# Complex products moved to GpSimd, constants set in the first stage, and an up product with stationary weights, in a two-layer state space, attention and mixture kernel

## What is computed

```
# 1. state space tokens: x holds C (8 batches x 256 channels x 64 states, complex)
dtA = A * dt[:, None];  dA = (1 + dtA/2) / (1 - dtA/2)
K   = 2 * Re( einsum('chn,hnl->chl', C * B, dA ** arange(256)) )
# 2. attention with causal mask, 3. attention and a mixture of experts by position,
# 4. gated linear attention, each with a layer norm behind it
# 5. mixture of experts: 8 experts, the best 2 for each token
h      = relu(x @ W1[e] + b1[e])           # 256 -> 1024
expert = h @ W2[e] + b2[e]                 # 1024 -> 256
out    = sum over the top 2 of expert * softmax(the two gate scores);  layernorm(x + out)
```

## Time and profile before

| what | value |
|---|---|
| median of 3 runs | 1494.32 us (1494.07 to 1497.88) |
| profiled execution, its own time | 1494.08 us |
| span of that execution | 1492.3 us |
| PE busy | 1115.6 us (75% of the span) |
| DVE busy | 695.7 us (47%) |
| ACT busy | 490.5 us (33%) |
| POOL busy | 144.6 us (10%) |
| mean granted TensorE clock | 0.833 of full speed |
| `s4_tokens`, from the start to the next block | 0 to 116.0 us |
| `main_loop` | 116.0 to 1029.9 us |
| main loop's constants | GpSimd 116.0 to 123.5 us, DVE 122.4 to 128.1 us |
| `expert_mixture` | 1029.9 us to the end; its 39 tiles from 1117 to 1436 us |

### The profile page before, as it was taken

The page is one execution under the profiler, slowest core; times in us unless marked ns, Lnnn a source line. Parts: engine busy times, 40 slices in busy tenths (PEclk is TensorE's granted clock), DMA queues, the critical chain, the costliest instruction groups (busy, mean ns, idle before and its releaser), DMA issues. The chain is left out here.

```text
span 1492.3 us, 21826 instructions
## 1 busy us (share of the span) xinstructions
PE 1115.6 (75%) x7926; PEld 745.1 (50%) x7926; DVE 695.7 (47%) x1686; ACT 490.5 (33%) x989; POOL 144.6 (10%) x211
## 2 busy tenths in 40 slices
PE   1134977987988888988879886773309999999940
PEld 0022655544764456763547554643306676676630
DVE  6972345664535766457674664243302222222227
ACT  2211232444543533454435442420002323333310
POOL 3741000000000000000000000000160000000035
PEclk9566896986989987899869987975559999999975
DMA  8011010000022000020001100103940101101114
GB/s 259 15 34 48 15 51 22 16 15 1 2 64 70 1 15 15 29 92 1 1 15 63 58 1 15 57 0 135 380 162 22 36 29 36 36 29 36 33 53 127
DMA packets 65480, 77.99 MB, mean 52 GB/s; under 512 B 14961, under 2 KB 57601, under 8 KB 65249
## 3 DMA queue, kind: packets, MB, share of 16 engines
q1 hardware_dynamic: 61040, 63.08, 13.2%
q0 software_dynamic: 4336, 13.50, 2.8%
HBM read 55.86 MB, written 20.71 MB: 51 GB/s over the span
## 5 line engine op out<-in xcount | busy, mean ns | idle before, releaser
L1463 DVE TENSOR_REDUCE mx<-scores_ps 128x4 f32<-128x1024 f32 (+1 forms) x160 | 187.1, 1169 | 140.4 <-PE scores_ps L947 93.4
L1286 ACT ACTIVATE pt<-turned_ps 128x1024 f32<-128x1024 f32 (+1 forms) x160 | 157.9, 987 | 148.3 <-PE turned_ps L969 102.8
L1908 PE MATMUL x_ps<-x_w,x_xtT 128*128 x312 | 143.5, 603 | 0.9 <-ACT x_xtT L1948 0.6
L1919 PE MATMUL x_ps<-x_w,x_hT 128*128 x624 | 141.2, 379 | 2.1 <-ACT x_hT L1963 2.1
L2054 DVE COPY x_raw<-x_ps 128x512 f32<-128x512 f32 x78 | 54.0, 692 | 168.4 <-PE x_ps L1908 168.4
L1963 ACT ACTIVATE x_hT<-x_ps,x_b1c 128x128 f32<-128x128 f32 x312 | 85.0, 383 | 142.0 <-PE x_ps L1926 142.0
L1919 PEld LDWEIGHTS x_ps<-x_w,x_hT 128*128 128x128 f32 x624 | 115.6, 190 | 16.8 <-issue 2.7
L959 PE MATMUL turned_ps<-q,k 32*128 32x256 f32 x512 | 73.7, 363 | 25.4 <-DVE mx L1463 14.7
L897 POOL COPY vpad<-v 128x64 f32<-128x64 f32 x64 | 17.3, 301 | 743.2 <-PE ps L1008 597.5
L959 PEld LDWEIGHTS turned_ps<-q,k 32*128 32x128 f32 x512 | 45.8, 210 | 84.3 <-issue 48.3
L1908 PEld LDWEIGHTS x_ps<-x_w,x_xtT 128*128 128x128 f32 x312 | 57.3, 194 | 59.2 <-issue 59.2
(11 more groups left out here) (360 smaller groups left out, 1991.1 us busy)
## 6 DMA issues: line engine op xcount, KB each, us to landing
wexp<-in_L_ffn_w SPq DMA_DIRECT2D x16, 1024.0 KB, 5.5
x_w<-in_L_ffn_W SPq DMA_DIRECT2D x16, 1024.0 KB, 13.8
x_slots<-s_zero POOLq DMA_DIRECT2D x1, 4992.0 KB, 19.3
x_xt<-x_slots SPq DMA_DIRECT2D x39, 128.0 KB, 2.2
y_slots<-x_y SPq DMA_DIRECT2D x39, 128.0 KB, 1.7
ha<-h SPq DMA_DIRECT2D x16, 256.0 KB, 3.1
h<-s_out SPq DMA_DIRECT2D x32, 64.0 KB, 1.8
x<-hb SPq DMA_DIRECT2D x8, 256.0 KB, 2.5
```

What stands on the lines that cost most here:

```text
L1286: sc.activation(pt[v.index // 2 % (PT_RING // 2)][:, :, 0:wide], turned_ps[:, :, 0:wide], ACT.Exp)\
L1463: v.tensor_reduce(mx[:, u.group % 2, 0:blocks, u.n:u.n + 2].rearrange("p b n -> p n b"), scores_ps[:, :, 0:blocks * (P if u.causal else T) ...
L1908: last = mm(ps[h][:, :], xtT[:, i % 2, c, :], w1[:, bass.ds(expert, 1), c, h * HALF:(h + 1) * HALF], start=c == 0, stop=c == DC - 1)
L1919: last = mm(ps[4 + (i - 1) % 2][:, 0:D], hT[:, (i - 1) % 2, f, :], w2[:, bass.ds(last_expert, 1), f, :], start=f == 0, stop=f == FT - 1)
```

## The change

There are three parts.

**State space step.** DVE no longer makes the imaginary part of `cb`. It signals `discrete` when `da` is ready; TensorE turns the two blocks of `da` alone, and DVE reads the result from PSUM into `dk[0]` (the buffer `dat` is gone). GpSimd waits until all eight squares are there, doubles B, and makes both parts of `cb`; TensorE turns them four blocks at a time, and ACT copies four at once. The zero fill of the scatter buffer follows behind them. The last block of the output is stored by ACT instead of SP.

**Constants.** The class `Constants` holds the buffers; GpSimd fills them behind its last group of columns, DVE prepares weights and selection matrices behind its last group of powers. The buffer `v0[1]`, which shares its place with others, is still set in the main loop. The activation table is loaded at the start.

**Mixture.** DVE copies the 128 x 2048 values of the tile's `w1` into one of two buffers `w1s`, two tiles ahead. TensorE takes 128 x 128 blocks of it as stationary and the 128 columns of `xtT` as moving, so the up result comes out turned: 16 matmuls for a tile into banks 0 and 1, or 2 and 3. The 8 transposes and the copies to `raw` are gone, and ACT reads the up product's banks itself.

```diff
+    def by_vector(self, dve, v, ident, wt):
+        s = Counted(dve, self.steps)
+        dve.wait_ge(wt.loaded, 16 * len(wt.loads))
...
+        dve.wait_ge(self.in_place, 1)
...
+        dve.sem_inc(self.ready, 1)
@@ s4_tokens, gpsimd
             pool.wait_ge(loaded, 16 * NLOAD)
+            pool.wait_ge(x_loaded, 16 * HF)
+            pool.wait_ge(squares, 8)
             g_.tensor_scalar(bin_[:, :, :, :], bin_[:, :, :, :], 2.0, None, ALU.mult).then_inc(doubled, 1)
             pool.wait_ge(doubled, 1)
-            pool.wait_ge(x_loaded, 16 * HF)
-            s.mark(g_.tensor_tensor(cb_part(0), xr, br, ALU.mult))
-            s.step(g_.tensor_tensor(ct[0][:, :, :, :], xi, bi, ALU.mult))
-            g_.tensor_tensor(cb_part(0), cb_part(0), ct[0][:, :, :, :], ALU.subtract).then_inc(prepared, 1)
+            for i, (u, w, op) in enumerate(((br, bi, ALU.subtract), (bi, br, ALU.add))):
+                s.mark(g_.tensor_tensor(cb_part(i), xr, u, ALU.mult))
+                s.step(g_.tensor_tensor(ct[i][:, :, :, :], xi, w, ALU.mult))
+                g_.tensor_tensor(cb_part(i), cb_part(i), ct[i][:, :, :, :], op).then_inc(prepared, 1)
...
-            pool.wait_ge(squares, 8)
...
+            consts.by_pool(pool, g_, ident)
@@ s4_tokens, scalar, behind the last copy
+            n = HF * NG - 1
+            act.wait_ge(copied, n + 1)
+            for j in range(J):
+                t0 = P + (NG - 1) * GT + j * TI
+                act.dma_start(h0[t0:t0 + TI].rearrange("t c (a b) -> (c a) t b", b=NB),
+                              out[n % 4][j * M:(j + 1) * M, :, :]).then_inc(stored[n % 4], 16)
@@ expert_mixture, tensor
-                    if i:
-                        pe.wait_ge(sg("raw"), 2 * i)
-                    for h in range(2):
+                    pe.wait_ge(sg("w1_now"), i + 1)
+                    if i >= 2:
+                        pe.wait_ge(sg("hT"), FT * (i - 1))
+                    for f in range(FT):
                         for c in range(DC):
-                            last = mm(ps[h][:, :], xtT[:, i % 2, c, :],
-                                      w1[:, bass.ds(expert, 1), c, h * HALF:(h + 1) * HALF],
-                                      start=c == 0, stop=c == DC - 1)
-                        last.then_inc(sg("up_full"), 1)
+                            last = mm(ps[2 * (i % 2) + f // KH][:, f % KH * P:(f % KH + 1) * P],
+                                      w1s[:, i % 2, c, f * P:(f + 1) * P],
+                                      xtT[:, i % 2, c, :], start=c == 0, stop=c == DC - 1)
+                        if f % KH == KH - 1:
+                            last.then_inc(sg("up_full"), 1)
...
-                if i < TILES:
-                    for h in range(2):
-                        pe.wait_ge(sg("raw"), 2 * i + h + 1)
-                        for k in range(KH):
-                            last = tr(ps[2 + h][:, k * P:(k + 1) * P], raw[:, h, k * P:(k + 1) * P], ident[:, :])
-                        last.then_inc(sg("hT_full"), 1)
@@ expert_mixture, vector
+            def take_w1(i):
+                expert = dve.value_load(te[0:1, i:i + 1], min_val=0, max_val=E - 1)
+                if i >= 2:
+                    dve.wait_ge(sg("up_full"), 2 * (i - 1))
+                v.tensor_copy(w1s[:, i % 2], w1[:, bass.ds(expert, 1)].rearrange("p o c f -> p (o c) f"))\
+                    .then_inc(sg("w1_now"), 1)
+
+            take_w1(0)
+            take_w1(1)
+            for j in range(TILES):
+                if j + 2 < TILES:
+                    take_w1(j + 2)
```

More of the change, by code:

```diff
@@ L102, in s4_tokens @@
+def s4_tokens(nc, ctx, whole, x, log_dt, inv_a_real, a_imag, b_ri, h0, ident, xs, weights, consts):
     CH, HF, NB, NA = B, T // P, 64, 4
@@ L209, in _ @@
                 sp.dma_start(dst, src).then_inc(weights.loaded, 16)
-            for n in range(HF * NG):
+            for n in range(HF * NG - 1):
                 g, f = n // HF, n % HF
@@ L328, in _ @@
                 dve.sem_inc(powers, 1)
+            dve.wait_ge(constants, 2)
+            consts.by_vector(dve, v, ident, weights)
         @block.scalar
         def _(act):
-            for k in range(5):
-                act.wait_ge(transposed, k + 1)
-                for i in range(4 if k < 4 else 2):
-                    n = 4 * k + i
-                    dst = cbt[:, n // CH, n % CH, :] if n < 2 * CH else dat[:, n - 2 * CH, :]
-                    last = nc.scalar.copy(dst, ps[k][:, i * P:(i + 1) * P])
-                last.then_inc(columns, 1)
+            nc.scalar.preload_act_table_set("natural_log_exp_and_others")
             for k in range(6):
@@ L342, in _ @@
                 nc.scalar.copy(factor(k), dk[k][:, :, :]).then_inc(factors, 1)
+            for k in range(4):
+                act.wait_ge(transposed, k + 1)
+                nc.scalar.copy(cbt[:, k // 2, k % 2 * 4:k % 2 * 4 + 4, :],
+                               ps[3 + k % 2][:, :].rearrange("p (c t) -> p c t", c=4)).then_inc(columns, 1)
             def first_columns(g):
@@ L677, in done, with main_loop @@
         return self.freed[self.at[name, p]]
-def main_loop(nc, ctx, whole, io, h0, x3, ident, weights):
+def main_loop(nc, ctx, whole, io, h0, x3, ident, weights, consts):
     plan = Plan()
@@ L744, in main_loop @@
     sg = Signals(nc, ctx, "m")
-    constants, ready = sg("constants"), sg("ready")
-    N_CONST = 13
     def w_slot(p, i):
@@ L1250, in b_stream @@
                 yield from {"Y1a": y1a, "Y1b": y1b}[stage](p)
-        pe.wait_ge(ready, 1)
-        pe.wait_ge(constants, N_CONST)
-        pe.wait_ge(sg("ones_col"), 6)
+        pe.wait_ge(cn.ready, 1)
+        pe.wait_ge(cn.in_place, cn.N_POOL)
+        pe.wait_ge(cn.ones_col, cn.N_ONES)
         pe.wait_ge(sg("b1_in"), 16)
@@ L1414, in b_stream @@
                 yield from {"Y1a": y1a, "Y1b": y1b}[stage](p)
-        act.wait_ge(ready, 1)
-        sc.preload_act_table_set("natural_log_exp_and_others")
-        act.wait_ge(constants, N_CONST)
-        act.wait_ge(sg("ones_col"), 6)
+        act.wait_ge(cn.ready, 1)
+        act.wait_ge(cn.in_place, cn.N_POOL)
+        act.wait_ge(cn.ones_col, cn.N_ONES)
+        act.wait_ge(sg("early_v"), 2)
         act.wait_ge(sg("b1_full"), 1)
@@ L1761, in expert_mixture @@
     acc = sb("x_acc", [P, NTB, D])
-    xTr = sb("x_Tr", [P, 2, DC, GRP * P])
+    with ExitStack() as early:
+        xTr = early.enter_context(nc.sbuf_tensor("x_Tr", [P, 2, DC, GRP * P], fp32))
+    with ExitStack() as late:
+        pair = late.enter_context(nc.sbuf_tensor("x_pair", [P, GR, 2, D], fp32))
+    w1s = sb("x_w1s", [P, 2, DC, F])
     w1, w2 = sb("x_w1", [P, E, DC, F]), sb("x_w2", [P, E, FT, D])
     xt, xtT = sb("x_xt", [P, XR, D]), sb("x_xtT", [P, 2, DC, P])
-    raw = sb("x_raw", [P, 2, HALF])
     hT = sb("x_hT", [P, 2, FT, P])
     y = sb("x_y", [P, 2, D])
-    pair = sb("x_pair", [P, GR, 2, D])
     wg, bg = sb("x_wg", [P, DC, E]), sb("x_bg", [P, E])
```

212 lines of the change are left out of this document (107 added, 105 removed).

## The result

The changed kernel took 1454.83 us (median of 4 runs, 1452.88 to 1460.77), the kernel before 1496.1 us (4 runs, 1494.07 to 1505.4; three of them are those of the table before): a ratio of 0.972, 95% interval 0.967 to 0.977. The forecast was 1448.3 us, range 1439 to 1458. The profiled execution has a span of 1452.4 us where before it was 1492.3, so 39.9 us are gone and not the 45.8 of the sum.

The account below looks back on a forecast made before the run. TensorE was taken to bound the tiles, DVE the first block, and DVE's constants the seam; mixture 31.7, state space step 3.8, last stores 2.0 and constants 8.3 sum to 45.8 us, so 1494.1 becomes 1448.3 us, range 1439 to 1458.

Parts of the forecast that it names:

- state space step to k = 4: First block: DVE starts k = 4 of the first group at 46.5 instead of 50.31 us, a gain of 3.8 us.
- last stores: End of the state space step: ACT issues four of the last eight transfers beside SP, 2.0 us gained.
- constants: Seam to main loop: constants hidden in the first block, TensorE starts 3.95 instead of 12.24 us in, 8.3 us gained.
- scatter: Before the tiles: DVE's first two w1 copies fall into GpSimd's scatter, 1.2 us lost, between nothing and two copies.
- tiles and last down product: Mixture: 39 shorter tiles give 30.8 us, and the last down product's wait for relu goes, 2.1 us.
- close: Stretch from the last bias addition to the end; the prediction has no term for it.
- The up product: Mixture tiles: weight loads overlap products, 110 ns a record, 3.52 us a product, 0.08 more than before; tile 0.79 us shorter.
- The bound of 111.4: Up product: upper bound in ns for a record, from load-bound products with 64 moving columns; 107.5 was the lower.
- The last relu's wait: End of the tiles: the last down product's 2.06 us stop for relu behind the transposes goes, 2.1 us gained.
- (a): Rival, up product: loads wholly exposed, 215 ns a record, tile 2.6 us longer, 1580 us; chance 0.03.
- (b): Rival, up product: loads half exposed, 163 ns a record, tile 0.9 us longer, 1514 us; chance 0.04.
- Who could be late: Mixture: DVE's w1 copy takes 1.7 us a tile, at most 3.4, with some 4 us to spare; ACT not late.

Follow-up runs that it names:

- before_again: The kernel before, unchanged, run again on chip B for a second trace: 1491.83 us, ratio 1.000.
- half_columns: Changed kernel with 64 instead of 128 moving columns a record in the up product, half the last expert layer left uncomputed: 1452.73 us (one run).
- after_again: The changed kernel, unaltered, run again on chip A: 1455.94 us, ratio 0.970 to the kernel before.
- after_third: The changed kernel, unaltered, run a third time, on chip C: 1445.42 us, ratio 0.968 to the kernel before.
- stores_sp: Changed kernel with all of the state space step's stores issued by SP, none by ACT: 1441.98 us (one run).

## Where the prediction held, and where it didn't

The span fell by 39.9 us where the sum had 45.8. Term by term, before to after, from the first two lines of the table:

| term | predicted | measured |
|---|---|---|
| state space step to k = 4 | 3.8 | 5.3, of which 1.3 by an earlier start |
| last stores | 2.0 | 1.0 |
| constants | 8.3 | 8.0 at the first block, 9.7 over the loop |
| scatter | -1.2 | -1.5 |
| tiles and last down product | 32.9 | 32.1 |
| close | 0 | -6.5 |
| sum | 45.8 | 40.1, and 39.9 by the spans |

Without the close the measured terms come to 46.6 us, close to the 45.8 in part by luck: the last stores, the scatter and the tiles fell short by 2.1 us together, and an earlier start (1.3) and the main loop, 9.7 for 8.3, made up for it. The loads landed at 5.90 us in the trace of before and at 4.62 in the one after; before_again has 4.93, so most of this start is chance. Where both kernels ran on one chip at one time, their medians differ by 48.3 us (A) and 49.7 us (C, interval 45 to 52), against 41.3 in the first comparison, whose times of before are mostly older. So the change may be worth a little more than the forecast said, though the interval still holds it, and no run shows to which term the rest would belong.

- **The up product, right.** Loads overlap; the record is 111.6 ns, not 110, so a tile is 0.75 us shorter instead of 0.79. The bound of 111.4 from the products with 64 columns was nearly the answer, and half_columns shows why: it was the load's own price. Of two equal bounds I should have taken the upper one. The last relu's wait went as foretold: the last down product runs on without a gap (1382.55, 6.92 us for 32 records). Rivals (a) and (b), exposed loads, would need 215 and 163 ns a record and are out.
- **Who could be late, right by more than I knew.** DVE's copy of 2048 values is 1.23 us, not 1.7; pricing by proportion from one on 512 values was too dear.
- **Scatter, right.** 1.37 us on one transfer. Here and in half_columns the held transfer ends 0.12 us after the copies (1077.24 to 1077.12, 1079.06 to 1078.94). What is lost depends on where the transfers fall: 1.0 us in after_again, where the held one starts 0.6 us into the copies, and 1.5 us over two transfers in after_third. The 1.2 was a value chosen between the bounds of 0 and 3.4 us and fell near by luck.
- **State space step, right in its mechanism.** `da` at 12.75 (14.2 foretold, 1.3 of it the earlier loads), products of 2.82, 2.82 and 2.35 us beside DVE, the stop in front of ACT's copy of the first powers, the step ended by DVE. Taken without the earlier start, the lead is 4.0 us for 3.8.
- **Last stores, mis-sized.** 1.0 us for 2.0 (stores_sp). The step that failed is that four issues fewer on SP are 2 us less: the transfers themselves were the other bound that I had named, and they cut in half way, each landing 0.5 to 0.6 us later when two queues issue.
- **Constants, right.** The TensorE of the changed kernel starts 4.25 us into the loop, 3.95 foretold. It is idle in the loop for 150 us in ten traces with the constants moved and for 158 to 160 in three without. What was incomplete was my picture of what they cost: DVE's 5.7 us of work, but ahead of it also 6.4 us of waiting for GpSimd.
- **The close, not foreseen.** No step speaks of it, and by the runs none had to: the same kernel has 56.1 us on chip C and 63.9 on A.
- **The rest goes with TensorE's clock.** The loop varies from 902 to 912 us over kernels with the same instructions and the same 150 us idle; the rest of it is TensorE busy for 751.5 to 762 us. The two shortest have mean granted clocks of 0.86 and 0.87, the longest 0.85. That is the spread which hides gains of 2 or 3 us.

## To carry to other kernels

Making the expert's weights the stationary operand, and so getting the result already turned, cost TensorE only 0.13 us a tile here, because a record's 128 moving columns (107.5 ns) are about as long as the 110 ns that it takes in any case; with 64 columns half of TensorE's time would go unused. What has to be counted is the engine that must now copy or serve the weights. When one engine has long idle time in a pipeline of two arms, look how soon the other arm becomes the bound before spending on it: here 11 us of idle time were worth 2.8. And an edit that is to be undone in an experiment has to be undone with its waits, or it measures something else.

## What was not expected

A closing stretch of 56 us took 64 on one chip with each of the four kernels traced there, DVE waiting up to 3.28 us between instructions of its own with no releaser that the profile shows; a comparison across chips would have charged 8 us to the change. And small fp32 operations of DVE within SBUF are held up by one whole GpSimd instruction each, 2.45 to 2.90 us for 0.3, in the same way in which a transfer of the scatter waits for DVE's copies, while operations with an operand in PSUM are not.
